# Edge stages on tiles of 128 edges, with the running sums in two PSUM banks by parity

## The reference

```python
# first edge stage (continuous filter)
C = 0.25 * (cos(edge_weight * pi) + 1.0)
W = ssp(edge_attr_64 @ fw1.T + fb1) @ fw2.T + fb2        # per edge, 64 -> 256 -> 256
msg = (x @ w1.T)[src] * (W * C[:, None])
agg = segment_sum(msg, dst, 3125)

# second edge stage (attention over the edges of a node, 8 heads of 32)
q, k, v = split(h @ W_qkv + b_qkv)
score = einsum('ehd,ehd->eh', q[dst], k[src]) * SCALE
ex = exp(score - segment_max(score, dst)[dst])
attn = ex / segment_sum(ex, dst)[dst]
h_new = segment_sum(attn[:, :, None] * v[src], dst)
```

## Time and profile before

| | |
|---|---|
| median of 3 runs | 2128.72 us (2126.48 to 2131.48) |
| profiled execution, span from the first to the last instruction | 2134.3 us; no other time of this execution is recorded |
| TensorE, its weight loads | busy 83%, 72% of the span |
| VectorE, ScalarE, GpSimd | busy 72%, 50%, 54% |
| mean granted clock of TensorE | 0.903 of 2.4 GHz |
| preparation | 0 to 34 us |
| first edge stage | 81 to 791 us |
| nodes, experts, segments, projection | 791 to 1241 us |
| attention | 1241 to 1900 us |
| output, selection, feed-forward | 1900 to 2134 us |

### The profile page before, as it was taken

One profiled execution on the slowest core, in us unless ns is written; L12 is line 12 of the kernel. 1 busy time (PEld: TensorE's weight loads), 2 busy tenths in 40 slices (PEclk: granted clock), 3 DMA queues, 4 the chain that ended last, 5 costly groups with the idle time before them and its releaser, 6 DMA issues. The chain is left out here.

```text
span 2134.3 us, 41549 instructions
## 1 busy us (share of the span) xinstructions
PE 1761.5 (83%) x10388; PEld 1537.1 (72%) x10389; DVE 1539.6 (72%) x2788; ACT 1070.3 (50%) x2353; POOL 1160.5 (54%) x1169
## 2 busy tenths in 40 slices
PE   3699999999999989828973868888888888866278
PEld 3499999999999979728972756666666766645267
DVE  5388888888888845643545849899999898847622
ACT  1677777777777726403420145445455454316133
POOL 0376666666666601462443457777777777512112
PEclk7799999999999989758996989999999999867579
DMA  3443333333333312133323566666666666524310
GB/s 96 133 121 111 104 108 108 104 107 108 105 106 108 98 31 80 69 124 98 119 75 98 193 185 189 189 188 188 193 191 186 190 187 188 148 65 141 115 38 29
DMA packets 132538, 267.55 MB, mean 125 GB/s; under 512 B 24030, under 2 KB 75888, under 8 KB 132407
## 3 DMA queue, kind: packets, MB, share of 16 engines
q0 software_dynamic: 63456, 191.61, 30.7%
q1 hardware_dynamic: 68534, 73.21, 11.2%
q10 hardware_dynamic: 416, 1.18, 0.2%
HBM read 225.34 MB, written 42.50 MB: 125 GB/s over the span
## 5 line engine op out<-in xcount | busy, mean ns | idle before, releaser
L319 POOL DMA_INDIRECT e_rows<-h_table,e_idx x440 | 453.4, 1030 | 214.1 <-issue 106.3
L1740 POOL DMA_INDIRECT a_rows<-kv_table,a_idx x440 | 476.1, 1082 | 135.8 <-issue 128.9
L619 PE MATMUL e_w<-w2h,e_hidl 128*128 128x256 f32 x880 | 247.7, 304 | 2.9 <-DVE e_msg L704 2.9
L589 PE MATMUL e_agg<-e_msg,e_hot 128*128 128x256 f32 x880 | 246.1, 402 | 0.0
L1822 PE MATMUL a_q<-q,a_spread 128*128 x880 | 233.7, 407 | 6.5 <-ACT a_spread L1782 6.3
L620 PE MATMUL e_w<-w2l,e_hidh 128*128 128x256 f32 x880 | 226.4, 280 | 0.0
L1853 PE MATMUL a_agg<-a_rows,x 128*128 128x264 f32 x880 | 226.2, 402 | 0.0
L704 DVE TENSOR_TENSOR e_msg<-e_w,e_rows 128x1024 f32<-128x1024 f32 x110 | 134.7, 1224 | 93.4 <-PE e_w L623 93.4
L1775 ACT ACTIVATE a_apart<-iota_n,dst_rel 128x128 f32<-128x128 f32 x440 | 140.6, 391 | 112.9 <-PE a_agg L1853 112.8
L1822 PEld LDWEIGHTS a_q<-q,a_spread 128*128 128x128 f32 x880 | 166.2, 199 | 38.9 <-issue 12.8
L1853 PEld LDWEIGHTS a_agg<-a_rows,x 128*128 128x128 f32 x880 | 168.2, 200 | 24.7
(11 more groups left out here) (456 smaller groups left out, 4221.4 us busy)
## 6 DMA issues: line engine op xcount, KB each, us to landing
e_ea<-in_eaT SPq DMA_DIRECT2D x220, 64.0 KB
m_rows<-expert_rows SPq DMA_DIRECT2D x32, 272.0 KB, 2.7
e_rows<-h_table,e_idx POOLq DMA_INDIRECT x440
a_rows<-kv_table,a_idx POOLq DMA_INDIRECT x440, 3.7
q_ab<-expert_out SPq DMA_DIRECT2D x50, 128.0 KB, 3.3
kv_table<-q_kv SPq DMA_DIRECT2D x25, 256.0 KB, 2.2
u_stage<-in_m_w SPq DMA_DIRECT2D x16, 256.0 KB
x<-in_x SPq DMA_DIRECT2D x1, 3200.0 KB, 13.9
```

The source lines that it names most:

```text
L319: c.nc.gpsimd.indirect_dma_start(out=rows[:, g.slot8, j, :], out_offset=None, in_=table, in_offset=bass.IndirectOffsetOnAxis(ap=idx[:, g.s ...
L589: last = mm(bank(wins[j]), hot[:, g.slot4, t, :], msg[:, g.slot4, t, :], start=False, stop=False, skip_group_check=True)
L619: mm(w, hidl[:, g.slot, cols[k]], w2h[:, k, :], start=(k == 0), stop=False)
L1740: nc.gpsimd.indirect_dma_start(out=rows[:, g.slot * IG + j, 0:2 * D], out_offset=None, in_=c.kv_dram, in_offset=bass.IndirectOffsetOnAxis( ...
```

## The change

Tiles of 128 edges take the place of items of 256. There are 392 tiles (`NT`), which make 98 groups of four (`NTG`), and 392 + 24 = 416 (tile, window) pairs, which make 104 groups (`NIG`). In the first edge stage the messages are made once for each tile, in 98 groups, and stay in a ring of 14 groups (`rows`, which the product now overwrites); the sums run over the 104 groups and take each message from its slot in the ring, whose number is loaded at run time (`slots_of`). In attention everything runs over 104 groups. The four tiles of a group can lie in different windows, so their numbers are packed, 5 bits each (6 for slots), in one word, and unpacked with shifts and masks on each engine. TensorE adds two tiles at a time (`add_pair`), sending a product of two columns to the bank that is not the first tile's, and one to the bank that was not the last one's of the pair before; ScalarE copies twice per pair (`keep`), where the first copy goes to a spare window if both tiles have the same.

Attention gets the same scheme: the sums stay in two PSUM banks by parity, TensorE adds a pair at the end of a step and the second pair in the middle of the next, ScalarE copies them out, and VectorE no longer adds. The rescale is done on the PSUM bank. VectorE's order in a step is the message of group i - 6, the rescale, the product of group i. The hardware loop of the first stage and `Ahead` are gone; all steps are written out. GpSimd takes its indices straight from the prepared columns, without ScalarE's copy. The memset of `c.sums` ahead of attention is gone.

```diff
-NT = -(-(E + 1) // TE)
-NI = NT + NW - 1
-NC = NI * CT
+NT = RT * RC                       # RT, RC = 98, 4
+NC = NT + NW - 1
+NTG = NT // IG
 NIG = NC // IG
+LATE = -(-(NW - 1) // IG)
+RING = 14
...
+def unpacked(packed, bits, most):
+    return [((packed >> (bits * j)) & ((1 << bits) - 1)).with_bounds(min_val=0, max_val=most) for j in range(IG)]
+def windows_of(eng, c, n):
+    return unpacked(eng.value_load(c.g_row[0:1, n:n + 1], ...), W_BITS, NW - 1)
+# targets_of (c.k_row) and slots_of (c.s_row) likewise
...
 # prepare, VectorE (chained small operations on one partition)
+                for lo, hi, laps in lap_spans():
+                    last = v.tensor_scalar(turn[:, lo:hi], t_all[0:1, lo:hi], float(-laps * RING_T), None, ALU.add)
...
+                for n, (row, base) in enumerate(((w_all[0:1, :], W_BITS), (slot[:, :], S_BITS), (target[:, :], W_BITS))):
+                    link(v.tensor_copy(packed[:, n, :], row[:, 0:NC:IG]))
+                    for j in range(1, IG):
+                        link(v.scalar_tensor_tensor(packed[:, n, :], row[:, j:NC:IG], float(1 << (base * j)), packed[:, n, :], ALU.mult, ALU.add))
...
 # prepare, TensorE
+                for k in range(RC):
+                    last = nc.tensor.matmul(p_c[:, 3, k * RT:(k + 1) * RT], rows_f[:, 0, k, :], c.ident[0:RT, 0:RT], start=True, stop=True)
...
 # first edge stage, TensorE
-                def add_item(g, j, wins):
-                    need(pe, None, (s_msg, g.n + 1), (s_acc, g.n * JG + j), own=True)
-                    mm(other(wins[j])[:, 0:2], none[:, :], w2h[:, 0, 0:2], start=True, stop=False, skip_group_check=True)
-                    for half in range(CT):
-                        t = j * CT + half
-                        last = mm(bank(wins[j]), hot[:, g.slot4, t, :], msg[:, g.slot4, t, :], start=False, ...)
+                def add_pair(a, half, wins, slots):
+                    need(pe, None, (s_msg, min(a.n + 1, NTG)), (s_hot, a.n + 1), (s_acc, a.n * PAIRS + half), own=True)
+                    first = 2 * half
+                    if last_window[0] is not None:
+                        mm(other(last_window[0])[:, 0:2], none[:, 0:P], none[:, 0:2], start=True, stop=False, skip_group_check=True)
+                    mm(other(wins[first])[:, 0:2], none[:, 0:P], none[:, 0:2], start=True, stop=False, skip_group_check=True)
+                    for j in range(first, first + 2):
+                        last = mm(bank(wins[j]), hot[:, a.slot4, j, :], flat(rows[:, bass.ds(slots[j], 1), :]), start=False, ...)
                     last.then_inc(s_agg, 1)
...
 # first edge stage, ScalarE
-                    nc.scalar.copy(flat(c.sums[:, bass.ds(wins[j], 1), 0:D]), bank(wins[j])).then_inc(s_acc, 1)
+                    for j in (2 * half, 2 * half + 1):
+                        last = nc.scalar.copy(flat(c.sums[:, bass.ds(wins[j], 1), 0:D]), bank(wins[j]))
+                    last.then_inc(s_acc, 1)
...
 # attention, ScalarE, in this order in a step
+                    if real(Edges(i.n - LAG - 1)):
+                        keep(Edges(i.n - LAG - 1), 1, wins)
...
+                    if real(m):
+                        wins = targets_of(act, c, m.n)
+                        keep(m, 0, wins)
...
...
 # attention, TensorE
+                def add_pair(m, half, wins):
+                    rescaled = (s_rs, 2 * (m.chunk + 1)) if m.place == 0 and half == 0 else (s_rs, 0)
+                    need(pe, None, (s_msg, m.n + 1), (s_acc, PAIRS * m.n + half), rescaled, own=True)
...
+                        queries((0, 1))
+                    if real(b):
+                        add_pair(b, 1, sums)
+                    if i.place == 2 and closed(ch):
+                        move_ex(ch)
+                    if real(g):
+                        queries((2, 3)).then_inc(s_q, 1)
...
+                        sums = windows_of(pe, c, m.n)
+                        add_pair(m, 0, sums)
...
 # attention, VectorE
-                        v.tensor_tensor(to, to, ap[:, :, 0:DM], ALU.add).then_inc(s_acc, 1)
...
-                        need(dve, s_dg, (s_gr, ch + 1), (s_acc, i.n - LAG))
-                        v.scalar_tensor_tensor(to, grow..., 1.0, to, ALU.add, ALU.mult).then_inc(s_rs, 1)
+                        need(dve, s_dg, (s_gr, ch + 1), (s_acc, PAIRS * m.n))
+                        v.tensor_scalar(grown[:, :], grow, 1.0, None, ALU.add).then_inc(s_gw, 1)
+                        need(dve, s_dg, (s_gw, ch + 1))
+                        to = ap[:, bass.ds(w, 1), 0:D].rearrange("p a (h d) -> p (a h) d", h=H)
+                        v.tensor_tensor(to, to, grown[:, :]..., ALU.mult).then_inc(s_rs, 1)
```

More of the change, by code:

```diff
@@ L295, in need, with rounds @@
         eng.sem_inc(gate, 1)
-def rounds(eng, step, before, after, kind=Group):
+def rounds(eng, step, before, after, kind):
     size = kind.UNROLL
@@ L592, in step @@
-                def step(at):
-                    a = at(-1)
-                    if real(a):
-                        sums = item_windows(pe, c, a.n)
-                        add_item(a, 0, sums)
-                    g = at(5)
-                    if real(g):
-                        need(pe, None, (s_el, g.n + 1), (s_hid, g.n - 1), own=True)
+                for p in range(2):
+                    mm(ap[:, p, 0:D], none[:, 0:P], none[:, :], start=True, stop=False, skip_group_check=True)
+                last_window = [None]
@@ new lines, in add_pair @@
+                def add_pair(a, half, wins, slots):
[5 more added lines that the diff above has]
+                    for j in range(first, first + 2):
+                        last = mm(bank(wins[j]), hot[:, a.slot4, j, :], flat(rows[:, bass.ds(slots[j], 1), :]), start=False, stop=False, skip_group_check=True)
+                    last.then_inc(s_agg, 1)
+                    last_window[0] = wins[first + 1]
@@ L601, in step @@
+                for r in range(-5, NIG + 1):
+                    a, g, z = Group(r - 1, NIG), Group(r + 1), Group(r + 5)
+                    if a.real():
+                        wins, slots = windows_of(pe, c, a.n), slots_of(pe, c, a.n)
+                        add_pair(a, 0, wins, slots)
+                    if z.real():
+                        need(pe, None, (s_el, z.n + 1), (s_hid, z.n - 1), own=True)
                         for m in range(KC):
[L602 removed]
@@ L1746, in _, with keep @@
                 act.preload_act_table_set("natural_log_exp_and_others")
-                def step(at):
-                    i = at(0)
+                def keep(m, half, wins):
+                    need(act, s_ag, (s_agg, m.n * PAIRS + half + 1))
+                    for j in (2 * half, 2 * half + 1):
+                        last = nc.scalar.copy(flat(c.sums[:, bass.ds(wins[j], 1), :]), bank(wins[j]))
+                    last.then_inc(s_acc, 1)
+                wins = None
+                for i in steps:
+                    if real(Edges(i.n - LAG - 1)):
+                        keep(Edges(i.n - LAG - 1), 1, wins)
                     if i.place == 2 and closed(i.chunk - 1):
@@ L1845, in step @@
                     if real(m):
-                        need(pe, None, (s_msg, m.n + 1), (s_acc, m.n), own=True)
-                        mm(ap[:, 1, 0:DM], none[:, 0:P], none[:, 0:DM], start=True, stop=False, skip_group_check=True)
-                        for j in range(JG):
-                            to = ap[:, 0, 0:DM] if j == 0 else ap[:, bass.ds(moved, 1), 0:DM].rearrange("p a d -> p (a d)")
-                            for half in range(CT):
-                                t = m.slot * IG + j * CT + half
-                                last = mm(to, hot[:, t, :], rows[:, t, D:ROW], start=(j == 0 and half == 0), stop=False, skip_group_check=True)
-                        last.then_inc(s_agg, 1)
+                        sums = windows_of(pe, c, m.n)
+                        add_pair(m, 0, sums)
                     if i.place == 0 and closed(ch):
@@ L1879, in linked @@
                     return link
-                def step(at):
-                    i = at(0)
+                for i in steps:
                     ch = i.chunk - 1
-                    a = at(-LAG - 1)
-                    if real(a):
-                        w = ahead.take(i.step, "sums", a.n)
-                        need(dve, s_dg, (s_agg, a.n + 1), (s_acc, a.n), *([(s_rs, 2 * a.chunk + 2)] if a.place == 0 else []))
-                        to = c.sums[:, bass.ds(w, JG), :]
-                        v.tensor_tensor(to, to, ap[:, :, 0:DM], ALU.add).then_inc(s_acc, 1)
-                    m = at(-LAG)
+                    m = Edges(i.n - LAG)
                     if real(m):
```

448 lines of the change are left out of this document (203 added, 245 removed).

## The result

The changed kernel takes 2561.1 us (median of 4 runs, 2556.53 to 2564.31) against 2130.1 (4 runs, 2126.48 to 2132.22) for the kernel before on the same chip: ratio 1.202, 95% interval 1.1999 to 1.2041. The forecast was 2259, range 2150 to 2350. The sign was right and the size was off by more than three times.

A forecast was written before the change was run, and what follows sets the result against it. It took the TensorE-ScalarE round trip per pair as setting the changed kernel's pace. Terms -23 + 51 + 79 + 17 + 7.5 - 1 = +130.5 us, added to the median 2128.7, gave 2259 us, range 2150 to 2350.

The forecast's parts named there:

- perhaps 2 us more in a queue that now hides all of it: First stage, TensorE: upper end of the steady term, 7.2 us a group, from two loads and some forty address steps.
- address term of the cycle: Round trip between TensorE and ScalarE: address arithmetic adds 0.02 to 0.22 us to a cycle taken as 3.0.
- TensorE's sequencer becomes the bound: Rival: register work sets 7.2 us a group in both stages, 2366 us; chance 0.10 shared with the clock rival.
- First stage, steady part: First edge stage: 98 message groups at 6.68 us in place of 6.157 a group, -23 us.
- The 0.48 us from a copy's end to the next product: First stage's round trip: delay from ScalarE's copy end to TensorE's two-column product, counted as 0.48 us of each cycle.
- slack: Middle of the first stage: the round trip was hidden before the change with only 0.27 us to spare.
- First tail: End of first stage: twelve pairs at 4.15 us at the lower clock, with nothing in between; +51 us.
- Attention, steady part: Attention: two round trips of 3.0 us a group in series plus 0.65, 6.65 a group against 5.557; +79 us.
- Attention's tail: End of attention: thirteen cycles of 4.15 us and 6 for the last chunk, 60 against 42.6; +17 us.
- preparation: Before the first stage: a larger ranking product and more VectorE work, less a wait for x; +7.5 us.
- between the stages: Segments between the edge stages have 26 chunks for 28, worth 0 to 2 us; -1 us.
- low-end rival: Rival: all terms at their low ends, gain and handshake cancel, +4 us, 2132 us; chance 0.06.

The follow-up runs named there:

- constants on both: Changed kernel with constants in place of all register values on TensorE, and constant windows and banks for ScalarE's copies, in both edge stages: 2144.4 us, ratio 1.009.
- early unpacking: Changed kernel with values cut straight from the packed words, in blocks spread between TensorE's other products, and before ScalarE's wait: 2319.2 us, ratio 1.089.
- block moved: Changed kernel with unpacking spread between products, and attention's load and unpacking for the next queries moved ahead of the waits for scores and carries: 2257.3 us, ratio 1.061.
- filled waits: Changed kernel plus useless zero products where TensorE waits in attention: 2566.6 us; the same with spread unpacking and moved query block, both tails filled too: 2336.9 us.
- constants on TensorE: Changed kernel with constants in place of all register values on TensorE in both edge stages, ScalarE keeping its own: 2180.0 us, ratio 1.024.
- filled tails: Changed kernel with constants on TensorE and ScalarE, plus 8 useless zero products after each pair in both tails: 2123.0 us, ratio 0.998.

## Why the prediction was wrong

**The step that failed** is the one that let register work hide: "perhaps 2 us more in a queue that now hides all of it", and with it the address term of the cycle, 0.02 to 0.22 us. The amount was nearly right in the first stage: 23 steps more at 0.09 and a second load at 0.7 are about 2.7 us of sequencer a group. In attention, where 32 more are 2.9 us, nothing was added but the address term. The cover was wrong in two ways. First, the unpacking stands behind the wait and between the products of a pair, where little or nothing is queued. Second, the queue's lead is short, and the trace of before showed it. The sequencer's lines for the group of the earlier trace rows:

```profile
L337 PEldq TENSOR_LOAD <-g_row x1: 300/300/300, 401.2 to 401.2; - x1
L337 PEldq FUSED_REGOPS  x1: 157/157/157, 401.6 to 401.6; - x1
L589 PEldq FUSED_REGOPS  x1: 46/46/46, 402.5 to 402.5; - x1
```

The load is issued at 401.2 for a pair that executes at 402.81, a lead of 1.6 us, and its last address step is at 402.5. Of the lead 0.3 us is left, at a place where TensorE was 50.00 of 50 us busy. The prediction read no idle time in a stage that already loads and unpacks as plenty of room; it was the last 0.3 us of it. The rival "TensorE's sequencer becomes the bound" had the mechanism, but was priced at 7.2 us a group by an upper end that still let most of it hide.

**First stage, steady part.** Forecast -23, measured +116.7. Without register work (constants, or unpacking spread) it is 6.36 x 97 = 617, -54: with the register work out of the way the round trip is hidden there, and the forecast of 6.68 was wrong in that direction too. The 0.48 us from a copy's end to the next product contained address steps: in the tail of the run with constants on both, a pair of copies ends at 740.46 and the next product starts at 740.60, 0.14 later. Without these steps the slack was larger than 0.27.

**First tail.** Forecast +51, measured +59.5. Cycles of 4.4 to 4.8 us (953.91 to 958.29, and copies started at 957.16 and 961.96) for 4.15:

```profile
953.91 0.36 PE L598 MATMUL e_agg<-e_none 128*128 128x2 f32 x1 [1.58 <-ACT sums L646]
...
958.29 0.37 PE L598 MATMUL e_agg<-e_none 128*128 128x2 f32 x1 [1.48 <-ACT sums L646]
```

The lower clock, forecast for it, is there (granted 0.50, the level of 1.2 GHz); a cycle at this clock is 3.63 with early unpacking and 3.38 with constants on both (740.60 to 743.98). So here too the handshake was priced too dear, and the register steps more than made up for it.

**Attention, steady part.** Forecast +79, measured +229.6. The mechanism was right: twice a group in series, two longer intervals in eight. Undisturbed cycles are 3.36 in the changed kernel and, with the blocks out of the way, 2.53, less than the 2.86 to 3.06 forecast. Starts of a pair's products in the changed kernel, and with the block moved:

```profile
1631.64 1.15 PE L1798 MATMUL a_agg<-a_rows,x 128*128 128x264 f32 x4
1634.28 0.27 PE L1794 MATMUL a_agg<-a_none 128*128 128x2 f32 x1
1634.79 0.27 PE L1795 MATMUL a_agg<-a_none 128*128 128x2 f32 x1 [0.24 <-issue]
1635.00 1.19 PE L1798 MATMUL a_agg<-a_rows,x 128*128 128x264 f32 x4
```
```profile
1602.66 1.14 PE L1871 MATMUL a_agg<-a_rows,x 128*128 128x264 f32 x4
1604.93 0.27 PE L1867 MATMUL a_agg<-a_none 128*128 128x2 f32 x1
1605.06 0.27 PE L1868 MATMUL a_agg<-a_none 128*128 128x2 f32 x1
1605.19 1.15 PE L1871 MATMUL a_agg<-a_rows,x 128*128 128x264 f32 x4
```

From the first two-column product to the pair it is 0.72 us in the first and 0.26 in the second. With constants on both a group is 6.04 us, 622 in all, +16: near the low end of the prediction, 5.97. So the difference of some 210 us is register work again: 8.11 - 6.37 on TensorE, 6.37 - 6.04 on ScalarE, each times 103. Unlike in the first stage, no run got all blocks here under long products; they stand next to waits for scores, carries and transposes.

**Attention's tail, preparation, between the stages.** +26.6 for +17, +4.9 for +7.5 (the first product's start, 112.8 for 107.9), -8.9 for -1.

**The clock.** From 1500 to 1800 us of attention it was granted 0.85 on average for 0.98 before. The changed kernel does four query products in 2.00 us at some places (1809.47, right after the wait for the carries), and 1.03 at others. By these rows it is a part of attention's loss, but no run isolates it: filled waits raised it to 0.90 in the changed kernel, and what that gave back and what the added products cost can't be told apart. It also rises when register work goes (0.92 with constants on TensorE, nothing filled). In the first tail its price is shown, 14 us.

**What would have been.** With no register work on the two engines and filled tails the change comes out at 0.998 of the kernel before, no difference that can be told: 12 groups of messages less are worth 54 us in the first stage, and its own tails and attention's two round trips a group take that back. Its best form with real addresses here is 6% slower. The low-end rival ("gain and handshake cancel", +4) was nearest for everything but register work (+19 with constants and unfilled tails).

**Open.** What the 0.75 us a group are that stay in attention between the run with the moved block (7.12) and constants on TensorE (6.37). The waits of the former from 1500 to 1700 us, 28 groups, point at register work once more:

```profile
PE a_q L1907 <- issue: 13.7, 13, 1.4
PE a_misc L1898 <- issue: 6.0, 7, 1.3
```

That is 19.7 us, 0.70 a group, and the view of the run with constants on TensorE has no line of PE with "issue". The moved block now stands directly behind the unpacking of the second pair: 16 steps and a load in a row, from 1605.3 to 1607.4 in one step, while the last products queued ahead of it start at 1605.19 and the next at 1607.57. No run took this block apart from the other, nor from the clock (0.89 for 0.92). Why products of no use held the clock in one tail and not in the other is not known.

## What to carry to other kernels

Before adding register arithmetic to an engine that looks full, read the sequencer's lead: from the start of its load or last address step to the start of the product that uses it. Price a step by the distance of starts (0.09 us here), not by its duration (0.034), and a wait runs the lead down: what stands behind it in program order is paid, but for what products still queued cover. If addresses must be unpacked, put the loads and steps in small blocks between long products, ahead of the wait, and not two blocks in a row; the first two of these, with 30 steps a group for 38 in the first stage, took 304 us of 431 off here, with the same products and copies.

## What was not expected of the hardware

A load of a word with its follow-up steps holds TensorE's sequencer for about 0.7 us, though the load shows 0.30. Start of the load, of its follow-up and of the next line's first step (a semaphore wait at 507.9 lies before it):

```profile
L361 PEldq TENSOR_LOAD <-s_row x1: 303/303/303, 507.2 to 507.2; - x1
L361 PEldq FUSED_REGOPS  x1: 151/151/151, 507.6 to 507.6; - x1
L361 PEldq SEQ_ASSERT  x1: 18/18/18, 507.8 to 507.8; - x1
L598 PEldq ALU_OP  x2: 36/36/36, 508.0 to 508.1; - x2
```

Eight products of zeros after each pair kept the granted clock at 1.00 through a tail of 40 us in which it had been 0.50; in attention's tail they left it at 0.50. And TensorE's busy time grew with the register work: a pair's four products show 1.49 us in the changed kernel and 1.11 before and with constants, because gaps shorter than a product's modelled duration don't show: the four start 0.32, 0.48 and 0.32 us apart, each with a duration of 0.38 or 0.48. A busy share of 45.40 in 50 us therefore hid that the stage had lost a quarter of its rate (6.157 / 8.12 = 0.76).
